# Turning the normalised tiles by DMA and VectorE instead of TensorE, in a transformer layer followed by a graph layer

## What is computed

```
h  = ln(x) * (1 + scale1) + shift1        # scale, shift = cond @ Wln1 + bln1, one pair per batch
x  = x + attention(h; 16 heads of 32) @ Wo + bo
h  = ln(x) * (1 + scale2) + shift2
x  = x + gelu(h @ W1 + b1) @ W2 + b2      # 512 -> 2048 -> 512
x  = x + relu(self(x) + gat_0(x) + gat_1(x))
```

## Time and profile before

| what | value |
|---|---|
| median of three runs | 3050.7 us |
| the profiled execution | 3049.14 us, span from first to last instruction 3047.8 us |
| mean granted TensorE clock | 0.997 of full speed |
| TensorE busy | 2993.2 us, 98% of the span |
| VectorE busy | 2144.6 us, 70% |
| GpSimd busy | 1579.5 us, 52% |
| ScalarE busy | 1385.1 us, 45% |
| DMA queues | 455.32 MB in 174013 packets |

### The profile page before, as it was taken

The page is one execution under the profiler, slowest core; times in us unless marked ns, Lnnn a source line. Parts: engine busy times, 40 slices in busy tenths (PEclk is TensorE's granted clock), DMA queues, the critical chain, the costliest instruction groups (busy, mean ns, idle before and its releaser), DMA issues.

```text
span 3047.8 us, 42422 instructions
## 1 busy us (share of the span) xinstructions
PE 2993.2 (98%) x15850; PEld 2089.7 (69%) x15850; DVE 2144.6 (70%) x3627; ACT 1385.1 (45%) x2673; POOL 1579.5 (52%) x685
## 2 busy tenths in 40 slices
PE   7999999999999999999999999999999999999999
PEld 6887655555555555555555546788888888789998
DVE  5558889899998989999899988643333333235666
ACT  3221577666666666666667663321111111022332
POOL 0000489899998999999899994400000000102222
PEclk9999999999999999999999999999999999999999
DMA  7683798989999899898998977720111110311221
GB/s 236 204 250 125 174 196 192 200 187 204 206 196 203 186 201 206 193 209 190 200 206 190 202 168 226 244 85 1 42 42 42 42 42 16 111 65 63 86 81 67
DMA packets 174013, 455.32 MB, mean 149 GB/s; under 512 B 19045, under 2 KB 61157, under 8 KB 142672
## 3 DMA queue, kind: packets, MB, share of 16 engines
q0 software_dynamic: 32064, 232.54, 37.3%
q1 hardware_dynamic: 139938, 214.51, 23.0%
q10 hardware_dynamic: 1806, 5.56, 0.7%
HBM read 143.47 MB, written 75.50 MB: 72 GB/s over the span
## 4 chain that ended last, share of the span: by engine, by line
PE 64%; POOL 15%; DMA 14%; DVE 3%; issue 3%; ACT 2%; SPq 0%; POOLq 0%; DVEq 0%; ACTq 0%
DMA pt<-pt 12%; PE ps L1296 11%; PE ps L1283 11%; POOL pt L949 9%; PE ps L427 7%; PE ps L742 6%; PE ps L753 6%; PE ps L525 5%; PE ps L1851 4%; POOL pt L921 3%; PE ps L529 3%; PE ps L1868 3%; ACT pt L837 2%; PE ps L1888 1%; DMA x<-in_x 1%
## 5 line engine op out<-in xcount | busy, mean ns | idle before, releaser
L440 DVE TENSOR_REDUCE nmp<-ps 128x1 f32<-128x512 f32 x1966 | 1200.6, 681 | 58.8 <-PE ps L427 56.7
L837 ACT ACTIVATE pt<-ps 128x512 f32<-128x512 f32 x2048 | 1030.9, 629 | 447.9 <-PE ps L742 426.5
L949 POOL TENSOR_TENSOR pt<-pt 128x2048 f32<-128x2048 f32 x217 | 1099.4, 5066 | 11.1 <-ACT pt L837 6.4
L742 PE MATMUL ps<-qs,ks 128*128 128x512 f32 x2048 | 803.1, 396 | 5.0 <-ACT pt L837 4.9
L427 PE MATMUL ps<-ks,qs 128*128 128x512 f32 x1966 | 802.3, 408 | 0.1
L427 PEld LDWEIGHTS ps<-ks,qs 128*128 128x128 f32 x1966 | 368.8, 188 | 264.8 <-DVE nmp L440 172.6
L753 PE MATMUL ps<-pt,vq 128*32 128x512 f32 x4096 | 492.5, 598 | 0.0
L742 PEld LDWEIGHTS ps<-qs,ks 128*128 128x128 f32 x2048 | 383.6, 188 | 114.6 <-ACT pt L837 34.1
L1283 PE MATMUL ps<-hpb,w 128*128 128x512 f32 x1536 | 376.9, 395 | 0.0
L1296 PE MATMUL ps<-w,gp 128*128 128x512 f32 x1536 | 369.3, 389 | 3.0 <-DVE gp L1412 3.0
L1296 PEld LDWEIGHTS ps<-w,gp 128*128 128x128 f32 x1536 | 288.1, 188 | 64.1 <-DVE gp L1412 4.3
(11 more groups left out here) (180 smaller groups left out, 2801.0 us busy)
## 6 DMA issues: line engine op xcount, KB each, us to landing
pt<-pt POOLq DMA_DIRECT2D x219, 1024.0 KB, 9.7
qk_d<-st SPq DMA_DIRECT2D x128, 256.0 KB, 2.9
qs<-qk_d SPq DMA_DIRECT2D x87, 256.0 KB
ks<-qk_d SPq DMA_DIRECT2D x42, 512.0 KB, 5.7
xina<-in_x SPq DMA_DIRECT2D x8, 1024.0 KB, 6.7
v_d<-vst SPq DMA_DIRECT2D x32, 256.0 KB, 2.6
vq<-v_d SPq DMA_DIRECT2D x32, 256.0 KB, 8.2
ao_d<-accs SPq DMA_DIRECT2D x32, 256.0 KB, 3.2
```

The lines of the kernel that those rows point to most:

```text
L440: dve.tensor_reduce(nmp[:, n // 4, n % 4:n % 4 + 1], ps[:, ring.bank["max", u], :], AX.X, ALU.max, negate=True).then_inc(s_mr, 1)
L742: pe.matmul(ps[:, score_bank(n), :], ksb[w % 2][:, hh, 128 * kt:128 * kt + 128], qsb[:, v % 3, hh, :], start=True, stop=True).then_inc(s_s ...
L837: act.activation(pt[:, exp_slot(g), hh, :], ps[:, score_bank(n), :], ACT.Exp, scale=SCALE).then_inc(s_exp, 1)
L949: pool.tensor_tensor(accumulator(v, 0), accumulator(v, 0), pt[:, exp_slot(g), :, :], ALU.add).then_inc(s_add, 1)
```

## The change

Chunk 0 of both norms is turned as before. Chunks 1 to 7 of both are turned in another way. After the scaling, SyncE issues 16 DMAs from SBUF to SBUF (`sp_parts`), one for each pair of a block pb of 32 rows within each 128-row tile and a block fb of 32 features within each quarter: each moves 32 partitions x 16 runs of 32 floats into `parts`. Then VectorE makes one instruction of 32 x 32 transposes per quarter (`dve_square`, 128 x 512) from `parts` into `turned`; for the second norm `turned` is `xinb` itself. `act_turn` reads `turned` in place of the PSUM bank.

The places move too. In QKV stats are all at j 0 and scale all at j 1, `sp_parts` is at j 2 ahead of that tile's stores, `dve_square` and `dve_turn` are at j 7 to 10, `act_turn` at j 7 to 10. In FF the load of `xinb` is at f 1 ahead of the four loads of `res`, stats and scale at f 3, `sp_parts` at f 4, `dve_square` ahead of `dve_gelu(q + 1)` and `dve_turn` behind it at f 9 to 12.

```diff
+    def sp_parts(self, ci):
+        sp, c = self.sp, self.first + ci
+        sp.wait_ge(self.s_norm, NK * (c + 1))
+        sp.wait_ge(self.s_turn, NK * c)
+        for pb in range(4):
+            for fb in range(4):
+                sp.dma_start(self.parts[32 * fb:32 * fb + 32, :, pb, :],
+                             self.xin[32 * pb:32 * pb + 32, :, :].rearrange("i t (k f) -> i (t k) f", f=128)
+                             [:, :, 32 * fb:32 * fb + 32]).then_inc(self.s_parts, 16)
+
+    def dve_square(self, ci, k):
+        dve = self.dve
+        dve.wait_ge(self.s_parts, self.part_count(ci))
+        dve.transpose(self.turned[:, k, :].rearrange("p (t s) -> p t s", t=NK),
+                      self.parts[:, :, :, :].rearrange("p (t k) b f -> p t k (b f)", k=NK)[:, :, k, :]
+                      ).then_inc(self.s_turn, 1)
+
+    def act_turn(self, ci, k, bank=None):
...
+        src = self.turned[:, k, :] if bank is None else self.ps[:, bank, :]
+        act.activation(self.hf[:, k % 2, :], src, ACT.Identity, bias=self.sc1[:, w, 1, k, b:b + 1],
...
@@ pe_qkv
-                    if 4 <= j < 8 and ci + 1 < NC8:
-                        fa.pe_turn(ci + 1, j - 4, j % 2)
@@ act_qkv
-                for j in range(8):
-                    if j >= 4 and ci + 1 < NC8:
-                        fa.act_turn(ci + 1, j - 4, j % 2)
+                for j in range(11):
+                    if j >= 7 and ci + 1 < NC8:
+                        fa.act_turn(ci + 1, j - 7)
+                    if j >= 8:
+                        continue
@@ dve_qkv
+                    if ci + 1 < NC8:
+                        if j == 0 and ci:
+                            fa.dve_stats(ci + 1, range(NK))
+                        elif j == 1 and ci:
+                            fa.dve_scale(ci + 1, range(NK))
+                        elif 7 <= j < 11:
+                            fa.dve_square(ci + 1, j - 7)
...
+                    if 7 <= j < 11 and ci + 1 < NC8:
+                        if j == 7 and ci:
+                            dve.wait_ge(s_vm, 4 * ci)
+                        fa.dve_turn(ci + 1, j - 7)
@@ sp_qkv
+                    if j == 2 and ci + 1 < NC8:
+                        fa.sp_parts(ci + 1)
@@ pe_ff
-                if 8 <= f < 12 and ci + 1 < NC8:
-                    fb.pe_turn(ci + 1, f - 8, 6 + f % 2)
@@ dve_ff
-                    if f == 5:
+                    if f == 3:
                         fb.dve_stats(ci + 1, range(NK))
                         fb.dve_scale(ci + 1, range(NK))
-                    if 8 <= f < 12:
...
+                    if 9 <= f < 13:
+                        fb.dve_square(ci + 1, f - 9)
                 if q + 1 < NQ:
                     dve_gelu(q + 1)
+                if ci + 1 < NC8 and 9 <= f < 13:
+                    if f == 9 and ci:
+                        dve.wait_ge(s_f1, NF * ci)
+                    fb.dve_turn(ci + 1, f - 9)
@@ sp_ff
                 if f == 1:
+                    if ci + 1 < NC8:
+                        sp.wait_ge(fb.s_hf, NK * (fb.first + ci + 1))
+                        sp_load_x2(ci + 1)
...
-                if f == 2 and ci + 1 < NC8:
-                    sp.wait_ge(fb.s_turn, NK * (fb.first + ci + 1))
-                    sp_load_x2(ci + 1)
+                if f == 4 and ci + 1 < NC8:
+                    fb.sp_parts(ci + 1)
```

More of the change, by code:

```diff
@@ L121, with __init__ @@
 class Front:
-    def __init__(self, nc, sems, which, xin, hf, hp, shared):
+    def __init__(self, nc, sems, which, xin, hf, hp, parts, turned, s_parts, shared):
+        self.sp, self.parts, self.turned, self.s_parts = nc.sync, parts, turned, s_parts
         self.pe, self.act, self.dve, self.pool = nc.tensor, nc.scalar, nc.vector, nc.gpsimd
@@ L167, in pe_turn, with part_count @@
         m.then_inc(self.s_turn, 1)
-    def act_turn(self, ci, k, bank):
+    def part_count(self, ci):
+        return 256 * ((NC8 - 1) * self.which + ci)
+    def sp_parts(self, ci):
[14 more added lines that the diff above has]
+    def act_turn(self, ci, k, bank=None):
         act, q, w, b = self.act, NK * (self.first + ci) + k, self.which, ci // NCH
@@ L174, in act_turn @@
             act.wait_ge(self.s_lo, q - 1)
-        act.activation(self.hf[:, k % 2, :], self.ps[:, bank, :], ACT.Identity, bias=self.sc1[:, w, 1, k, b:b + 1],
+        src = self.turned[:, k, :] if bank is None else self.ps[:, bank, :]
+        act.activation(self.hf[:, k % 2, :], src, ACT.Identity, bias=self.sc1[:, w, 1, k, b:b + 1],
                        scale=self.sc1[:, w, 0, k, b:b + 1]).then_inc(self.s_hf, 1)
@@ L253, in program @@
         hpa0 = take("hpa0", [128, 2, NK, CH], F32R)
-        fa = Front(nc, fsems, 0, take("xina", [128, NK, D]), take("hfa", [128, 2, CH]), [hpa0, hpa1], shared)
+        xina, hfa = take("xina", [128, NK, D]), take("hfa", [128, 2, CH])
         wtmp = take("wtmpa", [128, 4, D])
@@ L261, in program @@
         cond4 = take("cond4", [128, NK, 32])
+        s_parts = sem("s_parts")
+        fa = Front(nc, fsems, 0, xina, hfa, [hpa0, hpa1], take("partsa", [128, NK * NK, 4, 32]), take("turna", [128, NK, CH]),
+                   s_parts, shared)
+        assert cursor[0] <= top - 32768
         s_cz = sem("s_cz")
@@ L648, in sp_load_x @@
         def sp_load_x(ci):
-            if ci:
-                sp.wait_ge(fa.s_turn, NK * ci)
+            if ci == 1:
+                sp.wait_ge(fa.s_turn, NK)
+            elif ci:
+                sp.wait_ge(s_parts, fa.part_count(ci - 1))
             sp.dma_start(fa.xin[:, :, :],
@@ L1027, in program @@
         hpb1 = take("hpb1", [128, 2, NK, CH], F32R)
-        fb = Front(nc, fsems, 1, xinb, hfb, [hpb0, hpb1], shared)
+        partsb = place("partsb", [128, NK * NK, 4, 32], top - 10240)
+        fb = Front(nc, fsems, 1, xinb, hfb, [hpb0, hpb1], partsb, xinb, s_parts, shared)
         s_a3 = [sem(f"s_a3{i}") for i in range(3)]
@@ L1262, in program @@
         n_cw = 32 * NC8 + 16
-        s_cw_o1, s_small, s_x40, s_rz = sem("s_cw_o1"), sem("s_small"), sem("s_x40"), sem("s_rz")
+        s_cw_o1, s_small, s_x40, s_rz = s_parts, sem("s_small"), sem("s_x40"), sem("s_rz")
         (s_xT, s_xTc, s_nz, s_nzm, s_nzb, s_prep, s_qt, s_qtc, s_kvm, s_kv, s_rowm, s_rhi,
@@ L1392, in act_ff @@
                     ci, f = divmod(q - 1, NF)
-                    if 8 <= f < 12 and ci + 1 < NC8:
-                        fb.act_turn(ci + 1, f - 8, 6 + f % 2)
+                    if 9 <= f < 13 and ci + 1 < NC8:
+                        fb.act_turn(ci + 1, f - 9)
                 if q < NQ:
@@ L1477, in dve_ff @@
                 if ci + 1 < NC8:
-                    if f == 5:
+                    if f == 3:
                         fb.dve_stats(ci + 1, range(NK))
                         fb.dve_scale(ci + 1, range(NK))
-                    if 8 <= f < 12:
-                        if f == 8 and ci:
-                            dve.wait_ge(s_f1, NF * ci)
-                        fb.dve_turn(ci + 1, f - 8)
+                    if 9 <= f < 13:
+                        fb.dve_square(ci + 1, f - 9)
                 if q + 1 < NQ:
                     dve_gelu(q + 1)
+                if ci + 1 < NC8 and 9 <= f < 13:
+                    if f == 9 and ci:
+                        dve.wait_ge(s_f1, NF * ci)
+                    fb.dve_turn(ci + 1, f - 9)
                 if q < 12:
@@ L1662, in pe_vw @@
             pe.wait_ge(s_cw_o0, n_cw)
-            pe.wait_ge(s_cw_o1, 16)
+            pe.wait_ge(s_cw_o1, 256 * 2 * (NC8 - 1) + 16)
             for q in range(WG):
```

## The result

The kernel after takes 3085.5 us (median of 5 runs, 3080.58 to 3093.16) against 3049.1 before (median of 5 on the same chip). The ratio is 1.0121, 95% interval 1.0107 to 1.0135: slower, where I had forecast 3041 and a range of 3028 to 3060. It is rival (b), for which I had worked out 3083. All three signs that I had named for being wrong are there: issues over 9 us a chunk, ScalarE waiting for stores of `st` at j 6, and TensorE waiting for `hp` at j 0.

What follows compares the result with a forecast made beforehand. TensorE, 98% busy, was taken to pace QKV and FF except where VectorE does. Turns removed -25.0, QKV delays +9.3 and FF stall +6.3 gave -9.4 us: 3039.7, or 3041 as median, range 3028 to 3060.

Steps and rivals of the forecast that it cites:

- rival (b): QKV: transfers cost too much, over about 8 us a chunk delays evictions and the next chunk; 3083 us, chance 0.21.
- The 16 transfers of a chunk: SyncE in QKV: 16 transfers take 7 us (0.43 each), bounds 5.8 and 14.4 us.
- The Trainium skill's rule: DMAs below 512 bytes read, modify and write; doubling the 7 us gives 14, the upper bound.
- So the cover is about 1 us: QKV: 7 us of transfers are hidden, with about 1 us to spare around tile 6's eviction and the first square.
- The turns, -11.3 in QKV: TensorE in QKV: 23 turns that count are removed at 0.49 us each, 11.3 us gained.
- The squares: VectorE at j 7 to 10: 0.7 us each, rounds of 2.7 us, hidden in chunks 1 to 4.
- Chunk 5, "+3 (0 to 6)": QKV chunk 5: squares and turns beside the maxima on VectorE, and late pieces, cost 3 us.
- Chunk 6, "+2": QKV chunk 6: four added squares where VectorE paces, and scaling waiting for GpSimd, cost 2 us (0.5 to 3).
- FF, -13.7 + 6.3 = -7.4: FF: 28 turns removed gain 13.7 us; a stall ahead of chunk 0's `pe_ff2(4)` and low clock cost 6.3 (3 to 8).
- The sum: Whole kernel: -25.0 + 9.3 + 6.3 = -9.4 us, from 3049.14 to 3039.7 for the profiled execution.

Runs made afterwards that it cites:

- few: Kernel after, but chunks 2 to 7 of the first norm issue 4 transfers instead of 16, the other 12 blocks left out: 3055.4 us, 1.0018.
- issues_alone: ff_rest plus 16 unread transfers per chunk at j 2 of QKV, all stats and scaling at j 0 and 1, first norm turned by TensorE: 3066.8 us.
- stats_early: Kernel before, with only QKV's stats all moved to j 0 and scaling all to j 1: 3047.8 us, 0.9991.
- few_halves: As few, but QKV's stats and scaling by halves at j 0 to 3 and the transfers at j 4: 3070.6 us, 1.0069.
- ff_only: First norm as in the kernel before, second norm as in the kernel after: 3042.3 us against 3049.9, ratio 0.9979.
- ff_rest: Kernel before, with only chunks 2 to 7 of FF turned the new way, loads, stats and scaling in old places, transfers at f 6: 3037.1 us, 0.9960.
- ff_later: As ff_only, but FF's xinb load, stats and scaling in their old places and the 16 transfers at f 6: 3040.3 us, 0.9970.
- pool: Kernel after, but in QKV GpSimd's queue issues all 16 transfers instead of SyncE: 3092.9 us, 1.0154.

## Why the prediction was wrong, step by step

**The failed step is "The 16 transfers of a chunk. ... I take 7 us (0.43 each)".** It measured 10.7 us (0.63 each, median) in a quiet chunk and up to 18.9 beside other loads, 14.0 in the mean of the seven chunks. The working went wrong in two places. I took the price from landing times (condT, bln, v_d) although what holds up the stores behind is the time of the issue on SyncE, and the issue row that I did use, v_d's 0.36 us, is of another kind, SBUF to DRAM. The row for SBUF to SBUF, 0.58 us, was in the same trace. Second, I let the maximum of 2.4 us for one issue speak for rival (b) only as a bound, and didn't price the chunks that have such traffic one by one. That rival (b)'s 3083 comes so near is in part luck: its 14.4 us a chunk were 0.9 us for each landing in all seven chunks, while the mean of 14.0 is made of four chunks at 10.7 to 12.2 and three at 16.9 to 18.9, and the seventh lost nothing.

**The Trainium skill's rule was not what cost.** A piece of 128-byte runs landed in 2.1 us and its issue took no longer than that of 512-byte runs (0.63 against 0.60). The rule of the Trainium skill, page DMA: Bandwidth & Descriptors, section Specifications, on transfers below 512 bytes shows in none of these numbers; that the mean of 14.0 us meets the 14 that I had worked out from it is chance. Transfers large enough to show it in bandwidth were not tried.

**"So the cover is about 1 us" was nearly right, and the consequence too.** In chunk 2 ScalarE stood 4.09 us with issues of 10.71, so 6.6 us of issues would have been covered, not 8: its cover was gone at 7 already. TensorE, behind its banks, waited 2.29 and 3.41 us in chunks 2 and 3, so for it 8.4 and 7.3 us were covered, near the 8 of rival (b). By that rival's rule each us of issue over 8 is lost: (12.15 + 18.85 + 10.71 + 10.69 + 18.31 + 16.88) - 6 x 8 = 39.6 us over chunks 0 to 5. TensorE's added waits measure 42.6. What the rule leaves out is the 12.5 us of the clock behind them. I had left the clock out in QKV, though I counted it in FF.

**The turns, -11.3 in QKV.** Nearly right where nothing hides it: few's chunks 2 to 4 gain 1.4 to 1.7 of 1.96 us, and FF's chunks 1 to 6 1.98 each.

**The squares.** 0.7 us predicted, 0.704 measured, with rounds of 2.66 us.

**Chunk 5, "+3 (0 to 6)".** It lost 13.7 us. issues_alone loses 16.2 there without any square, some 6.5 of it by a wait that the kernel after hasn't, so the other 9.7 are in the main held stores. In the kernel after itself one wait of 11.88 us for VectorE follows VectorE's 12.30 us for a store. My cause (VectorE beside the maxima) was the small part. Even 4 transfers leave 10.6 us there, when the query loads run. few's trace shows what released ScalarE, a store that took 3.48 us to issue and 8.7 to land. Why that store was so slow stays open, since stats_early excludes the moved stats only and few_halves shifted part of the loss to chunk 4.

**Chunk 6, "+2".** It gained 1.6 us, from the moved stats and scaling alone (stats_early: the same 1.6).

**FF, -13.7 + 6.3 = -7.4.** The medians of ff_only give -7.6. The stall came where predicted:

```profile
2031.24 5.46 PE L1334 MATMUL ps<-w,gp 128*128 128x512 f32 x12 [4.75 <-DVE w L568]
...
2077.57 2.88 PE L1334 MATMUL ps<-w,gp 128*128 128x512 f32 x12
2083.01 2.88 PE L1334 MATMUL ps<-w,gp 128*128 128x512 f32 x12
```

4.75 us of idle time against 5.2, and 5.46 us for the tile against 2.88, 2.6 more where I had counted 1.1 for the clock: 7.4 for 6.3. The steps with turns now take 5.44 us, as forecast. In the profiled executions FF as a whole gained only 2.4 us (736.4 to 734.0). Chunks 1 to 6 gain 11.9. Chunk 0 loses 7.9, where 7.4 less its four turns makes 5.4: it has 1.8 us more by its fourth tile of `pe_ff1`, ahead of the stall. ff_rest has these 1.8 too though it leaves chunk 0 alone, and issues_alone, with the same FF, hasn't, so they seem to vary from execution to execution. Chunk 7, which has no turns in either kernel, took 1.6 more.

**The sum.** Of -9.4 forecast for the profiled execution +44.0 came (3093.16 less 3049.14): QKV +43.7 for -2.0, FF -2.4 for -7.4, and 2.7 elsewhere. The median of runs is 7.6 us below this execution of the kernel after, where I had added 1.6 to that of the kernel before.

## What to carry to other kernels

A DMA has two prices, its landing and the time that the issuing queue needs; what is queued behind it pays the second, so take it from a row of the same direction and multiply it by the count before anything else. When a transfer shares a queue with stores that free slots, the cover is the ring's slack in that queue, and it must be looked up in the busiest chunk, not in a normal one. Loads that stand behind the issues come late as well (the weights in ff_later). An eviction that comes late is harmless while PSUM banks cushion it, but not when the next stage's operands are made behind it on the same engine: then undo the part that lies there (the first norm and FF's chunk 0) and keep the rest, here 0.40% faster.

## What the runs showed of the hardware

- Issuing a DMA from SBUF to SBUF took SyncE 0.60 to 0.64 us (medians) in seven shapes of 16 KB to 64 KB; from SBUF to DRAM 0.32 to 0.36 us when free. GpSimd needed 0.65 us (pool).
- Beside other loads one issue took SyncE up to 4.57 us, and 16 took 18.9 us instead of 10.7. GpSimd's issues took at most 0.94 us each, but it stood between them (8.62 us ahead of one), so that 16 took it 15.5 us in chunk 1.
- After seven waits of 2.3 to 11.9 us in QKV (kernel after) TensorE's granted clock was 0.50 for 3.2 to 5.5 us of its work each, 28.3 us in sum. After three others, of 3.6, 3.0 and 1.7 us, it stayed at 1.00.
- A transpose of 32 x 32 blocks over 128 x 512 float32 took VectorE 0.70 us, as much as another float instruction of that size.
